# Storing the high and the low parts of precombined weight sums by separate transfers, with two buffers for the low parts

## The reference

```
attn: y = xn + ssm_scan(rmsnorm(xn, scale1))        # a linear recurrence along the tokens, 16 states per channel
      h = rmsnorm(y, scale2)
      out = y + gelu(h @ w1 + b1) @ w2 + b2         # 512 -> 2048 -> 512
ffn:  xq = fp4(xn), wq = fp4(w)                     # blocks of 16 values share a scale
      out = fp4(silu(xq @ wg.T) * (xq @ wu.T)) @ fp4(wd).T    # 512 -> 1408 -> 512
```

## Time and profile before

| | us |
|---|---|
| median of 3 runs | 3198.1 |
| lowest and highest | 3197.61 and 3199.45 |
| the profiled execution, whole | 3199.24 |
| its span, from the first to the last instruction | 3197.4 |
| PE busy, share of the span | 3016.1, 94% |
| mean granted TensorE clock | 0.983 |

### The profile page before, as it was taken

How to read it: one execution, slowest core, us unless ns; L and a number is a source line. 1 busy time by engine, 2 the same in 40 slices (tenths; PEclk the granted TensorE clock), 3 DMA queues, 4 the chain that set the end, 5 groups by cost and what they waited for, 6 DMA issues and landing times. The chain is left out here.

```text
span 3197.4 us, 44061 instructions
## 1 busy us (share of the span) xinstructions
PE 3016.1 (94%) x14525; PEld 2427.6 (76%) x14525; DVE 2179.4 (68%) x4455; ACT 1156.7 (36%) x1930; POOL 1599.9 (50%) x1457
## 2 busy tenths in 40 slices
PE   5899999999999999999999666899999999999999
PEld 3677878888877777777777445687888787878787
DVE  8799898887777767677776555656565656565622
ACT  5345665544544433434323322322222222222220
POOL 7556666655555555455553444345353545353413
PEclk9999999999999999999999878999999999999999
DMA  4133334357766666666545457777867686868541
GB/s 125 48 90 101 108 107 117 103 149 184 187 166 170 172 159 159 176 154 160 150 92 135 125 149 195 197 207 172 211 172 199 180 209 163 222 160 217 141 132 50
DMA packets 975794, 488.77 MB, mean 153 GB/s; under 512 B 689232, under 2 KB 817488, under 8 KB 973008
## 3 DMA queue, kind: packets, MB, share of 16 engines
q1 hardware_dynamic: 975568, 485.96, 58.4%
HBM read 346.84 MB, written 138.97 MB: 152 GB/s over the span
## 5 line engine op out<-in xcount | busy, mean ns | idle before, releaser
L1019 PE MATMUL bank<-XT,Wg 128*128 128x512 f32 (+1 forms) x2148 | 525.3, 394 | 6.3 <-DVE Wd L1371 6.3
L1019 PE MATMUL bank<-XT,Wu 128*128 128x512 f32 (+1 forms) x2148 | 516.4, 390 | 15.3 <-DVE sg L1304 14.8
L1041 PE MATMUL bank<-Wd,HT 128*128 128x512 f32 x2112 | 515.8, 393 | 6.5 <-POOL HT L2115 5.2
L1019 PEld LDWEIGHTS bank<-XT,Wu 128*128 128x128 f32 x2148 | 402.3, 190 | 105.2 <-issue 24.1
L2107 POOL TENSOR_TENSOR qa<-qb,qs 128x512 f32<-128x512 f32 (+2 forms) x277 | 308.1, 1113 | 344.2 <-DVE qb L1364 341.8
L1041 PEld LDWEIGHTS bank<-Wd,HT 128*128 128x128 f32 x2112 | 392.5, 188 | 105.7 <-issue 15.4
L1019 PEld LDWEIGHTS bank<-XT,Wg 128*128 128x128 f32 x2148 | 399.8, 191 | 94.7 <-DVE Wd L1371 8.3
L1215 PE MATMUL bank<-Wp,G 128*128 128x512 f32 x1800 | 456.9, 391 | 5.3 <-POOL G L2226 5.2
L1193 PE MATMUL bank<-HC,Wp 128*128 128x512 f32 x1680 | 423.5, 391 | 2.8 <-POOL WH L2219 2.8
L1215 PEld LDWEIGHTS bank<-Wp,G 128*128 128x128 f32 x1800 | 336.9, 188 | 79.7 <-POOL G L2226 10.5
L1193 PEld LDWEIGHTS bank<-HC,Wp 128*128 128x128 f32 x1680 | 316.8, 189 | 68.7 <-POOL WH L2219 3.2
(11 more groups left out here) (199 smaller groups left out, 4435.6 us busy)
## 6 DMA issues: line engine op xcount, KB each, us to landing
Wp<-r_A SPq DMA_DIRECT2D x392, 256.0 KB, 3.4
px<-in_L_attn_x_dram SPq DMA_DIRECT2D x128, 256.0 KB, 3.3
xin<-in_L_attn_x_dram SPq DMA_DIRECT2D x128, 256.0 KB, 3.4
sT<-r_K SPq DMA_DIRECT2D x128, 256.0 KB, 4.2
r_Z<-xin SPq DMA_DIRECT2D x64, 256.0 KB, 2.4
r_U<-ub SPq DMA_DIRECT2D x16, 1024.0 KB, 6.7
sU<-r_U SPq DMA_DIRECT2D x32, 512.0 KB, 5.1
r_Y<-sY SPq DMA_DIRECT2D x16, 1024.0 KB, 5.5
```

What stands on the lines that cost most here:

```text
L1019: ins = e.matmul(bk[:, 0:n], W[wh][:, k, :], inputs(xh, w, k), start=(k == 0 and p_ == 0), stop=(k == KD - 1 and p_ == 2))
L1041: ins = e.matmul(DNB[t % 4][:], HT[hh][:, w % 2, a * P:(a + 1) * P], Wd[wh][:, f, :], start=(w == first(n) and p_ == 0), stop=(w == last(n ...
```

## The change

`combine_store` is taken apart. The store of the high part is issued one step earlier in SP's program, right after the step in which ACT computes it and ahead of the next load of w1; the store of the low part stays where it was. The high stores count up d_wa alone; the low stores count up two semaphores d_wb, which are those of two finished transfers (d_cs and d_rs), by the parity of k. wl becomes two buffers taken in turn; the second, wl1, lies where st and s1 lie, which are used only later. `combine_high` now waits for the high stores and for the low part of the round before (which reads wh), and `combine_low` waits for the low store two rounds before. Whoever needed all stores now waits on d_wa and both d_wb, and the first `conv_turn`, which writes st, waits for the last low store from wl1.

```diff
@@ wl as two buffers
+        with ExitStack() as later:
+            wl1 = sbt(later, "wl1", [P, 8, P], F32R)
         st = sbt(mctx, "st", [P, D])
         s1 = sbt(mctx, "s1", [P, D])
...
-        wl = sbt(mctx, "wl", [P, 8, P], F32R)
+        wl = [sbt(mctx, "wl0", [P, 8, P], F32R), wl1]
...
+        d_wb = [d_cs, d_rs]
@@ SP
-            def combine_store(k):
-                u, kt = k // 2, k % 2
-                for h in range(2):
-                    e.wait_ge((s_wah, s_wal)[h], (WAH0, WAL0)[h] + k + 1)
-                    e.dma_start(bass.AP(r_A.tensor, u * 8 * P * 512 + 256 * h + P * kt, [[512, P], [P * 512, 8], [1, P]]),
-                                (wh, wl)[h][:].bitcast(F32)).then_inc(d_wa, 16)
+            def store_sums_high(k):
+                e.wait_ge(s_wah, WAH0 + k + 1)
+                e.dma_start(sums_place(k, 0), wh[:].bitcast(F32)).then_inc(d_wa, 16)
+
+            def store_sums_low(k):
+                e.wait_ge(s_wal, WAL0 + k + 1)
+                e.dma_start(sums_place(k, 1), wl[k % 2][:].bitcast(F32)).then_inc(d_wb[k % 2], 16)
...
                 for k in combine_steps(n - 2):
-                    combine_store(k)
+                    store_sums_low(k)
                 for k in combine_steps(n - 1):
+                    store_sums_high(k)
                     combine_load(k + 2)
@@ DVE, conv_turn
+                elif i == 0:
+                    e.wait_ge(d_wb[1], WB_0 + 16 * 8)
@@ ACT, combine_high
                 if k:
-                    e.wait_ge(d_wa, WA_0 + 32 * k)
+                    e.wait_ge(d_wa, WA_0 + 16 * k)
+                    e.wait_ge(s_wal, WAL0 + k)
@@ POOL, combine_low
                 e.wait_ge(s_wah, WAH0 + k + 1)
-                e.tensor_tensor(wl[:], wt[:, k % 2], wh[:].bitcast(F32), ALU.subtract).then_inc(s_wal, 1)
+                if k >= 2:
+                    e.wait_ge(d_wb[k % 2], WB_0 + 16 * (k // 2))
+                e.tensor_tensor(wl[k % 2][:], wt[:, k % 2], wh[:].bitcast(F32), ALU.subtract).then_inc(s_wal, 1)
```

More of the change, by code:

```diff
@@ L48 @@
 WSC0, WSUM0, WAH0, WAL0, HT0 = 4 * NST, 4 * NST, 3, 4, 11
-RING_0, OQ_0, ZQ_0, WT_0, Q_0, WA_0, QO_0 = 32, 16, 8 * NT, 16, 16, 16, 16
+RING_0, OQ_0, ZQ_0, WT_0, Q_0, WA_0, WB_0, QO_0 = 32, 16, 8 * NT, 16, 16, 16, 16, 16
 QUADS = ((0, 1), (2, 3), (4, 0), (1, 2))
@@ L753, in combine_load, with sums_place @@
                             ).then_inc(d_wt[k % 2], 16)
-            def combine_store(k):
-                u, kt = k // 2, k % 2
-                for h in range(2):
-                    e.wait_ge((s_wah, s_wal)[h], (WAH0, WAL0)[h] + k + 1)
-                    e.dma_start(bass.AP(r_A.tensor, u * 8 * P * 512 + 256 * h + P * kt, [[512, P], [P * 512, 8], [1, P]]),
-                                (wh, wl)[h][:].bitcast(F32)).then_inc(d_wa, 16)
+            def sums_place(k, h):
+                return bass.AP(r_A.tensor, k // 2 * 8 * P * 512 + 256 * h + P * (k % 2), [[512, P], [P * 512, 8], [1, P]])
+            def store_sums_high(k):
[4 more added lines that the diff above has]
+                e.dma_start(sums_place(k, 1), wl[k % 2][:].bitcast(F32)).then_inc(d_wb[k % 2], 16)
             def ring_load(q):
@@ L766, in ring_load @@
                     e.wait_ge(s_w1, 17 + q)
-                    e.wait_ge(d_wa, WA_0 + 32 * 4)
+                    e.wait_ge(d_wa, WA_0 + 16 * 4)
+                    for i in range(2):
+                        e.wait_ge(d_wb[i], WB_0 + 16 * 2)
                 e.dma_start(ring(q).bitcast(F32), r_A[q // 7 % 8, STEPS[q % 7][0]]).then_inc(d_ring[q % 14], 16)
@@ L1988, in conv_high @@
                     e.wait_ge(s_w1, 24)
-                    e.wait_ge(d_wa, WA_0 + 32 * 16)
+                    e.wait_ge(d_wa, WA_0 + 16 * 16)
+                    for j in range(2):
+                        e.wait_ge(d_wb[j], WB_0 + 16 * 8)
                     for j in range(4):
```

## The result

The changed kernel took 3144.5 us (median of 4 runs, 3141.06 to 3147.94) beside 3197.9 of the kernel before, over four runs: a ratio of 0.9836, with a 95% interval of 0.9819 to 0.9853. Timed once more, later, it took 3150.0 (3145.95 to 3152.93) beside 3199.9, 0.9846 (0.9832 to 0.9859). The change saves 50 to 53 us; the forecast was 68. The stated range, 3109 to 3149, holds for the first median and is missed by 1 us by the second. The first profiled execution of the changed kernel took 3141.06 us, the lowest of its runs, with a span of 3139.3; that of before, 3199.24, was near the highest of its own (3199.45), so the two spans differ by 58.1, more than the medians.

What follows compares the result with a forecast made beforehand. ACT, waiting for the previous round's store, was taken to bound the second stage: 222.4 - (74 + 77) = 71.4, less 2 for conv_turn, gives 69 us, so 3130 from 3199.2. Range 3109 to 3149 (0.62); 8 in 10, 3106 to 3165.

Steps and rivals of the forecast that it cites:

- First half: Second stage, rounds 0 to 8: 109.7 us would become 74, a gain of 36.
- the walk: Rounds 0 to 3 traced by row durations: 25.8 us, 8.6 each, so 69 for eight, before 5 us added.
- Second half: Second stage, rounds 8 to 15: 112.7 us would become 77, seven tile turns at 11 us, a gain of 36.
- the ring of zl: Second half: r_Q store, its landing, next zl load, POOL, next store; 9.5 us a turn, taken as 11.
- The wait in conv_turn: End of second stage: DVE's first transpose into st waits for the last low store; 2 us added, bounds 0 and 5.7.
- The waits on SP: SP's queue in the second stage: waiting for wh before the high store was said to cost nothing that shows.
- The floor of 138 us: PE's time for the second stage's 20 steps if its clock stays at 0.80, instead of 108.8; closes gains above 84.
- Rival 1: Second stage: SP's queue or full transfers replace the wait; gain 15 to 48, middle 32, 3167 us; chance 0.20.
- Rival 2: Second stage: PE's floor nearly reached; gain 90 to 105, about 3103 us; chance 0.12.
- Rival 3: Second stage: wh waits nearly as long for the next load of w1; no change, 3198 us; chance 0.02.
- Rival 4: SP stopped at the high store delays everything behind it; slower by 13, 3211 us; chance 0.02.
- The signs to look for: Second stage: wh waits under 3 us, rounds 8 to 10, PE idle 25, clock near 0.9, transfers 0.85 or more.

Runs made afterwards that it cites:

- e1: Changed kernel with the high store issued late again, right ahead of the low one; two low buffers and separate semaphores stay: 3187.2 us.
- e4: Changed kernel with a second zl tile for every other one of tiles 9 to 15, next r_Z load ahead of this tile's store: 3151.9 us.
- e3: Changed kernel with round 15's low store moved one step up, right behind its high store and ahead of the quarters' transfers: 3147.9 us.
- e11: Changed kernel with the high store issued by ACT from its own queue, right behind wh, no longer by SP: 3144.6 us.
- e8: Changed kernel with two zl tiles and SP's loads of xl and yl issued a step later, together: 3143.7 us.
- e5: Changed kernel storing only four of each round's eight sums, the third stage reading those four, so part of the work is left out: 3137.0 us.
- e12: Changed kernel with two zl tiles, xl and yl loads a step later, the tile's r_Q store first in its step, and high store on ACT: 3136.1 us.

## Why the prediction came out as it did

**What bounds the kernel.** Right. The store behind which ACT stood was the path, and e1 shows that its early issue is what frees it.

**First half.** Right in size, and right in the walk for two rounds of three: rounds 1 and 2 were foretold 8.9 and 5.3 us after the ones before them and came at 8.8 and 5.0. In the timeline of the changed kernel (1761 to 1783) the high store is out before the low part is even begun, and round 2 waits for nothing but the low part of round 1:

```profile
1770.30 1.04 ACT L1994 ACTIVATE wh<-wt 128x1024 fp32r<-128x1024 f32 x1
...
1771.36 0.36 SPq L763 DMA_DIRECT2D r_A<-wh  x1
1772.81 2.38 POOL L2227 TENSOR_TENSOR wl<-wt,wh 128x1024 fp32r<-128x1024 f32 x1
...
1775.30 1.06 ACT L1994 ACTIVATE wh<-wt 128x1024 fp32r<-128x1024 f32 x1 [2.35 <-POOL wl L2227]
```

Round 3 came after 14.0 and not 11.6. SP issued its load of w1 on time (21.3 us after wh(0), foretold 21.8), but the load landed after 5.7 us and not 3.1, right behind two stores:

```profile
1781.43 0.63 SPq L767 DMA_DIRECT2D r_A<-wl  x1
...
1782.11 0.58 SPq L763 DMA_DIRECT2D r_A<-wh  x1
...
1782.73 1.34 SPq L754 DMA_DIRECT2D wt<-in_L_attn_w_dram  x1
...
1788.48 0.91 ACT L1985 ACTIVATE wt<-wt,vec 128x256 f32<-128x256 f32 x2 [1.70 <-DMA wt<-in_L_attn_w_dram]
```

The prediction had taken the 3.1 from a wait, which is no landing; the median landing of these loads was 3.1 before indeed, and 4.0 after. The 5 us that the prediction added "for transfers that meet others" had no row behind them, and they cover what the walk left out: the walk alone gives 69 for the eight rounds, measured are 74.7. That the term 74 came out so close is partly luck. ACT waited 9.6 us in two waits for a high store (3.9 before wh(5), 5.7 before wh(8)), under the 3 us a round foretold, and 9.6 in five for loads of w1; the loads were not the larger part.

**Second half.** Here a term of the sum was wrong in size: "Eight tiles are seven such turns ... I take 11 us a turn: 77". They took 95.4, 13.6 a turn. This is nearly the whole miss: counted along wh(0), wh(8), Q(8), Q(15), HC and product, the forecast's parts are 74 + 10.0 + 77 + 6.6 + 29.3 = 197, the measured ones 74.7 + 8.5 + 95.4 + 5.4 + 29.9 = 213.9, and the third term alone is 18 apart. I had priced a turn from one row, of 9.5 us, and that turn was one of those that lie a single step apart. `early_steps` puts tiles at distances of one and two steps by turns (15, 16, 18, 19, 21, 22, 24, 25 for their stores). The one-step turns took 9.3 to 13.5 us after the change, much as before it (9.5 to 14.6); the two-step ones took 18.4, 19.9 and 12.9 (29.8, 21.9 and 14.2 before). A turn of two steps holds one or two combine rounds as well, with their loads and waits, in the same SP order. The loads of w1 sort the turns: the three of the changed kernel that have one or two such loads in them took 13.5, 18.4 and 19.9 us, the four that have none 9.6, 9.3, 12.9 and 11.8. That the ring of zl alone sets the pace is refuted by e4: a second tile moved the wait to the next landing in SP's order.

**The wait in conv_turn.** +2 foretold; 2.7 by e3 at HC, none of it visible in the total.

**The waits on SP.** "The waits themselves cost nothing that shows" holds for SP's wait on wh (9.9 us in 4 waits over 1764 to 1940, longest 4.6), but e11 shows that the high store's place in SP's order costs 4 us in the first half. The sum has no term for it other than the 5 us put on.

**The clock.** 0.88 in the 16 rounds against the 0.9 foretold. The floor of 138 us for a clock that stays at 0.80 did not come into play: PE was busy 124.1 us for 474 matmuls, 125.7 for the 480 of 20 steps. The Trainium skill (TensorE: Matmul & The Clock Gate, HAM oscillation) has the clock fall back in each longer wait for data; the trace agrees, since it rises from 0.81 and 0.78 in the two halves to 0.91 and 0.86 with shorter waits and is no fixed cost of the stage.

**The rivals.** Rival 1 (3167, SP's queue or full transfers) named the right cause for the half that fell short, at twice its size; e8 and e11 show SP's part in it, e5 that bytes have a part but no bound, since the half did not follow them. Rival 2 (the floor of PE) fell: PE is idle for 37 us. Rival 3 showed as a remainder: loads of w1 are now ACT's largest wait, 32.8 us against 26.1, but beside the 98 us that the wait for the store lost. Its forecast, no change, is refuted. Rival 4 (SP held at the high store) is refuted by the 4.6 us of its longest wait, under the 8.7 that it wanted, and by the time.

**The signs to look for.** Seen: the waits of the first half, POOL waiting for zl<-r_Z and DVE for zl in the second, 3.94 us of DVE before st. Seen in the first half only: rounds of 8 to 10 us (9.3, then 12.2 in the second, which is the prediction's sign for rival 1). Missed: PE idle 25 (37), a transfer share of 0.85 (0.80). So the range held, but narrowly: the first half was as forecast, the second was what rival 1 described.

**Open.** What sets the second half of the changed kernel is not one thing. Removing waits in SP's order (e8, e12) and shortening the transfers (e5) each bring 5 to 11 us of the stage, and no experiment took both away at once. How much of e12's floor is the transfers' share of 0.96 was not tried.

## What to carry to other kernels

When a buffer's reuse waits for a store, look at when that store is issued before adding buffers: here issuing it one step sooner was worth 39 us of a stage and the second buffer 20, yet that buffer only 6 without the sooner issue. Price a ring from all of its turns and from where the program puts them, not from its shortest one. In a queue that issues in order, two waits for landings that come together can hide each other, so that taking one away shows nothing; try them as a pair before calling either harmless.

## What the runs showed of the hardware

Of two stores of 512 KB issued close behind each other, the second takes longer to land. Before, that was the low one (5.2 us in the median, the high one 4.2). In the changed kernel 8 of the 16 high stores are issued within 1.6 us of a low one's issue, and they landed after 4.9 to 6.2 us, each later than its low store (3.5 to 4.9); the shortest landings of a high store, 3.2, are three issued 2.5 to 5.1 us behind one. The medians (last column below) have changed places. The mean of the two medians stayed at 4.7, though the stretch moves 204 GB/s and not 157. In e12 the transfers reached 248 GB/s at a share of 0.96, so for this mix of transfers a full share is some 258 GB/s (an estimate, 248 / 0.96).

```profile
r_A<-wh SPq DMA_DIRECT2D x16, 512.0 KB, 5.0
r_A<-wl SPq DMA_DIRECT2D x16, 512.0 KB, 4.3
```

Issuing the high store occupied ACT's queue for 0.37 to 0.39 us in e11, and SP's for 0.36 to 1.34 in the changed kernel.
